# Turning 28 of 64 attention items in 32x32 blocks on VectorE, with the blocks carried through DRAM

## What is computed

```python
q_big = apply_rope(einsum('bshk,hkq->bshq', layernorm(x) @ Wq.T, w_kc_q), sin_q, cos_q)
kv_r = apply_rope(kv_c, sin_k, cos_k)
q_r = einsum('bshq,hqr->bhsr', q_big, W_qr)
k_r = einsum('bld,hdr->bhlr', kv_r, W_kr)
attn = softmax(einsum('bhsr,bhlr->bhsl', q_r, k_r), axis=-1)
ctx_c = einsum('bhsl,bld->bhsd', attn, kv_r)
ctx = einsum('bhsd,hkd->bhsk', ctx_c, w_kc_kv)       # then @ Wo.T, gate, add to x
```

## Time and profile before

| | value |
|---|---|
| median of three timed runs | 262.97 us |
| span of the profiled execution, first to last instruction | 261.0 us |
| TensorE busy | 248.7 us, 95% |
| VectorE busy | 180.5 us, 69% |
| ScalarE busy | 144.0 us, 55% |
| GpSimd busy | 136.6 us, 52% |
| share of the chain that ended last: TensorE, VectorE, GpSimd, DMA, ScalarE | 79%, 6%, 5%, 4%, 3% |

### The profile page before, as it was taken

How to read it: one execution, slowest core, us unless ns; L and a number is a source line. 1 busy time by engine, 2 the same in 40 slices (tenths; PEclk the granted TensorE clock), 3 DMA queues, 4 the chain that set the end, 5 groups by cost and what they waited for, 6 DMA issues and landing times.

```text
span 261.0 us, 5668 instructions
## 1 busy us (share of the span) xinstructions
PE 248.7 (95%) x1961; PEld 187.1 (72%) x1961; DVE 180.5 (69%) x435; ACT 144.0 (55%) x440; POOL 136.6 (52%) x221
## 2 busy tenths in 40 slices
PE   6998999999999999999999999999999999889993
PEld 6874777587776878587857876787668758666871
DVE  3799889468775858386847774777658556676575
ACT  2720566574466454746445636656655477758551
POOL 3535139642782278525744565458624952527542
PEclk9999999999999999999999999999999999999997
DMA  6986542534100250124200300030003000000112
GB/s 229 231 224 162 178 102 82 136 106 136 41 0 3 50 173 3 43 58 92 82 3 0 80 4 0 14 70 3 1 0 82 2 3 0 1 3 0 41 34 91
DMA packets 17852, 16.72 MB, mean 64 GB/s; under 512 B 5152, under 2 KB 16544, under 8 KB 17824
## 3 DMA queue, kind: packets, MB, share of 16 engines
q1 hardware_dynamic: 17184, 15.64, 22.7%
q10 hardware_dynamic: 640, 0.72, 0.9%
HBM read 11.11 MB, written 1.05 MB: 47 GB/s over the span
## 4 chain that ended last, share of the span: by engine, by line
PE 79%; DVE 6%; POOL 5%; DMA 4%; ACT 3%; issue 3%; ACTq 0%; DVEq 0%; POOLq 0%
PE ring L1124 23%; PE probs_t L1308 12%; PE scores L1297 9%; PE context L1341 9%; PE ring L1165 5%; PE ring L1090 4%; PE ring L1188 2%; PE ring L1184 2%; PE ring L1186 2%; PE ring L1151 2%; DMA w_kc_q_sb<-in_w_kc_q 2%; POOL roped L599 2%; DMA moved<-cross 2%; PE ring L1113 1%; ACT probs L775 1%
## 5 line engine op out<-in xcount | busy, mean ns | idle before, releaser
L669 POOL TENSOR_SCALAR probs<-probs,inv_sum 128x256 f32<-128x256 f32 x128 | 59.6, 478 | 87.6 <-DVE inv_sum L1028 87.5
L785 ACT COPY probs_t_sb<-probs_t 128x512 f32<-128x512 f32 x64 | 37.6, 588 | 57.7 <-PE probs_t L1308 57.7
L775 ACT ACTIVATE probs<-scores,neg_max 128x256 f32<-128x256 f32 x128 | 59.9, 478 | 4.0 <-DVE neg_max L1022 3.8
L599 POOL TENSOR_TENSOR roped<-roped,cross 128x512 f32<-128x512 f32 x30 | 37.8, 1281 | 11.5 <-DVE cross L866 11.4
L1022 DVE TENSOR_REDUCE neg_max<-scores 128x2 f32<-128x512 f32 x64 | 40.9, 680 | 2.2 <-PE scores L1297 1.9
L1124 PE MATMUL ring<-xn_hi,a_hi 128*128 128x512 f32 x96 | 40.7, 424 | 0.1
L1308 PE MATMUL probs_t<-ident,probs 128*128 128x128 f32 x256 | 40.4, 280 | 0.3 <-POOL probs L669 0.3
L1124 PE MATMUL ring<-xn_hi,a_lo 128*128 128x512 f32 x96 | 37.7, 393 | 0.0
L865 DVE TENSOR_TENSOR roped<-ring,rope_q_sb 128x512 f32<-128x512 f32 x48 | 32.8, 684 | 6.9 <-PE ring L1124 6.7
L1124 PE MATMUL ring<-xn_lo,a_hi 128*128 128x512 f32 x96 | 37.5, 391 | 0.0
L1308 PEld LDWEIGHTS probs_t<-ident,probs 128*128 128x128 f32 x256 | 28.7, 140 | 9.8 <-issue 2.2
(11 more groups left out here) (116 smaller groups left out, 464.3 us busy)
## 6 DMA issues: line engine op xcount, KB each, us to landing
moved<-cross SPq DMA_DIRECT2D x30, 128.0 KB, 2.3
wo_t_sb<-in_wo_t SPq DMA_DIRECT2D x4, 512.0 KB, 4.8
w_qr_sb<-in_w_qr SPq DMA_DIRECT2D x4, 384.0 KB, 4.3
wq_sb<-in_wq SPq DMA_DIRECT2D x3, 512.0 KB, 4.0
w_kc_q_sb<-in_w_kc_q SPq DMA_DIRECT2D x3, 384.0 KB, 4.6
x_sb<-in_x SPq DMA_DIRECT2D x3, 256.0 KB, 5.9
out<-x_sb SPq DMA_DIRECT2D x3, 256.0 KB, 2.2
wq_sb<-in_wq SPq DMA_DIRECT2D x2, 256.0 KB, 4.5
```

The costliest lines, as they stand in the source:

```text
L599: last = nc.gpsimd.tensor_tensor(roped[:, j, k, :], roped[:, j, k, :], cross[:, k, j, :], ALU.add)
L669: last = nc.gpsimd.tensor_scalar(e, e, inv_sum[:, i % 4, half:half + 1], 1.0, ALU.mult, ALU.mult)
L775: last = nc.scalar.activation(probs[:, i % E_BUFS, half, :], scores[:, i % 2, half, :], ACT.Exp, bias=neg_max[:, i % 4, half:half + 1], ac ...
L785: nc.scalar.copy(probs_t_sb[:, i % T_BUFS], probs_t[:]).then_inc(probs_t_ready, 1)
```

## The change

Of each quad of the first seven steps, the first pair (i mod 4 below 2, 28 items) is not turned on TensorE and not copied by ScalarE. Instead:

1. VectorE turns the item's 32x32 blocks within their 32 partitions, from `probs` into `x2_t` (there called `blocks_t`), one instruction of 128x512 elements, one loop after the item, right behind a reciprocal.
2. SyncE stores the pair's blocks, 512 KB, to a scratch in DRAM by four DMAs of 32 partitions each, in runs of 512 bytes.
3. When all four have landed, SyncE loads the 512 KB back by one DMA in runs of 2048 bytes, each block row now on the partition of its key, into the buffers of `probs_t_sb` that the pair would have had. There are two places in DRAM and two in `probs_t_sb`, taken in turn; from the third pair on the load also waits for the contexts that read its place before.
4. The context products wait for the load, and read their moving operand in runs of 32 elements.

```diff
+        def by_blocks(i):
+            return i % 4 < 2 and i < items - ITEMS
...
+            def send_blocks(q):
+                at = blocks_dram[q // 2 % 2].rearrange("c a (q x) -> q a c x", q=4)
+                sp.wait_ge(blocks_turned, turned_by_blocks(2 * q + 1))
+                for quarter in range(4):
+                    rows = blocks_t[BLOCK * quarter:BLOCK * (quarter + 1)]
+                    sp.dma_start(at[quarter], rows.rearrange("p c e h b -> p c (e h b)")).then_inc(blocks_out, 16)
+            def fetch_blocks(q):
+                done = turned_by_blocks(2 * q + 1) // 2
+                sp.wait_ge(blocks_out, 64 * done)
+                if done > 2:
+                    sp.wait_ge(context_ready, q - 3)
+                sp.dma_start(moved_probs[:, q // 2 % 2].rearrange("p k q e h b -> p k (q e h b)"),
+                             blocks_dram[q // 2 % 2].rearrange("(k r) a x -> (r a) k x", k=2)).then_inc(blocks_in, 16)
...
+                    if i >= 2 and by_blocks(i - 2) and i % 4 == 2:
+                        send_blocks(i // 2 - 1)
+                    pieces(steps[n][s][0])
+                    if i >= 3 and by_blocks(i - 3) and i % 4 == 3:
+                        fetch_blocks(i // 2 - 1)
...
+            def turn_blocks(i):
+                if i < 0 or not by_blocks(i):
+                    return
+                dve.wait_ge(probs_ready, i + 1)
+                if i >= 4:
+                    dve.wait_ge(blocks_out, 32 * turned_by_blocks(i - i % 4 - 1))
+                nc.vector.transpose(blocks_t[:, :, i % 2, :, :].rearrange("p c h b -> p h c b"),
+                                    probs[:, i % E_BUFS].rearrange("p h (c a) -> p h c a", a=BLOCK)
+                                    ).then_inc(blocks_turned, 1)
...
                     if i + 1 < items:
                         inverse(i + 1)
+                    turn_blocks(i - 1)
                     contexts_low(contexts_at(i))
...
             def turn_probs(i):
+                if by_blocks(i):
+                    return
                 pe.wait_ge(probs_ready, i + 1)
-                if i:
-                    pe.wait_ge(probs_t_ready, i)
+                if turned_by_array(i) > 1:
+                    pe.wait_ge(probs_t_ready, turned_by_array(i) - 1)
...
-                pe.wait_ge(probs_t_ready, 2 * q + 2)
+                if by_blocks(2 * q):
+                    pe.wait_ge(blocks_in, 8 * turned_by_blocks(2 * q + 1))
+                else:
+                    pe.wait_ge(probs_t_ready, turned_by_array(2 * q + 1))
```

More of the change, by code:

```diff
@@ L40 @@
 LEAD = 2
+BLOCK = 32
+KEY_BLOCKS = L // BLOCK
 NO_BANK = ("n", "c", "table", "move", "hand", "root", "gate", "take", "part", "pre", "half")
@@ L374, in by_halves, with turned_by_blocks, turned_by_array @@
             return i >= items - ITEMS // 2
+        def by_blocks(i):
+            return i % 4 < 2 and i < items - ITEMS
+        def turned_by_blocks(i):
+            return sum(1 for other in range(i + 1) if by_blocks(other))
+        def turned_by_array(i):
+            return i + 1 - turned_by_blocks(i)
         def half_of(i):
@@ L529, in _ @@
             first_swap = banks.index(("q", 0, 0, 1))
[L530 to L554, removed]
@@ new lines, in pieces @@
+            def pieces(slot):
+                for u, piece in slot:
+                    kind = piece[0]
+                    if kind == "q" and piece[2:] == (0, 1):
+                        sp.wait_ge(ring_free, freed[u])
+                        swap_quarters(sp, range(4) if piece[1] else (0, 1))
+                        if piece[1] == 0:
+                            late_loads()
+                            if last_merge("a", 0) <= first_swap:
+                                sp.wait_ge(ring_full, last_merge("a", 0))
+                                load_query_weights(sp, 1)
+                                load_key_weights(sp, 1)
+                        continue
+                    if kind not in ("a", "m", "o") or piece[1] + 1 == GROUPS or u + 1 != last_merge(kind, piece[1]):
+                        continue
+                    g = piece[1] + 1
+                    if u < first_swap:
+                        continue
+                    sp.wait_ge(ring_full, u + 1)
+                    if kind == "a":
+                        load_query_weights(sp, g)
+                        load_key_weights(sp, g)
+                    elif kind == "m":
+                        load_rank_weights(sp, g)
+                    else:
+                        load_output_weights(sp, g)
@@ new lines, in _ @@
+            pieces(before)
+            pieces(start)
+            for n in range(STEPS):
+                for s in range(ITEMS):
+                    i = n * ITEMS + s
+                    if i >= 2 and by_blocks(i - 2) and i % 4 == 2:
[3 more added lines that the diff above has]
+                        fetch_blocks(i // 2 - 1)
+                    pieces(steps[n][s][1])
+            pieces(after)
@@ L710, in pieces @@
                         act.wait_ge(ring_full, u + 1)
+                        if c == 0:
+                            act.wait_ge(blocks_out, 32 * turned_by_blocks(items - 1))
                         nc.scalar.copy(x2_t[:, c % 4:c % 4 + w].rearrange("p a d t -> p (a d t)"),
@@ L771, in exponentials @@
                 act.wait_ge(max_ready, i + 1)
-                if i >= E_BUFS:
-                    act.wait_ge(transposed, i - E_BUFS + 1)
+                if i >= E_BUFS and by_blocks(i - E_BUFS):
+                    act.wait_ge(blocks_turned, turned_by_blocks(i - E_BUFS))
+                elif i >= E_BUFS:
+                    act.wait_ge(transposed, turned_by_array(i - E_BUFS))
                 for half in range(2):
```

18 lines of the change are left out of this document (15 added, 3 removed).

## The result

The changed kernel takes 260.14 us in the median (259.31 to 261.6), the kernel before, run beside it, 262.98 (262.7 to 263.21): a ratio of 0.9887, 95% interval 0.9858 to 0.9915. It is faster by 2.84 us, not by the forecast 8.5. Executions more than 1.5% above the fastest of their kernel are left out of every ratio in this document, but not out of the medians. The profiled execution took 259.31 us, its span is 257.5.

A forecast was written before the change was run, and what follows sets the result against it. TensorE was taken as the bound from 34 to 222 us. 12.3 us removed, less 2.6 taken back and 1.2 waited, saves 8.5: 262.97 - 8.5 = 254.5 us, 8-in-10 range 250.8 to 262.8.

The forecast's parts named there:

- what GpSimd takes back: TensorE reaching items 3, 18, 48 and 49 and smaller places earlier, then waiting for GpSimd: 2.6 us lost.
- Removed from TensorE: On TensorE, 28 items lose four turns each, at 0.44 us per item: 12.3 us saved.
- Added to VectorE: 28 block turns at 0.68 us, 19.0 us in all; VectorE stays under TensorE, so no cost.
- The estimate of 1.24 us: Block turn on VectorE priced as four blocks by the skill page; would make the forecast 256.1 instead of 254.5 us.
- nothing queues behind that wait: On VectorE, each turn's wait for normalised rows was said to be already met, GpSimd working in order.
- Added to SyncE: Four stores and one load per pair in SyncE's queue, costed at nothing; risk: the transfer, some 2 us of queue.
- The round trip: From the reciprocal before a pair's second turn through turn, stores and load: 9.25 us, bounds 7.95 to 12.0.
- half is given back: Rival: round trip of 10.5 us, 5.6 us waits at third, sixth, tenth, thirteenth pairs' contexts; 258.9 us, chance 0.12.
- The thirteenth pair: Context products there, with a lead shrunk to 8.06 us, were the one costed wait for a load: 1.2 us.
- The range: 8-in-10 range for the whole kernel's time, leaving out slower cases and the fastest edge: 250.8 to 262.8 us.
- the forecast's own range: Likeliest case for the kernel's time: 252.3 (no load wait) to 257.6 us (round trip of 10.2); chance 0.58.
- The signs: Profile after: 144 TensorE turns, TensorE over 97% busy, turn near 0.68 us, one load wait near the thirteenth pair.

The follow-up runs named there:

- kernel 1: Against the kernel after: no block turns, stores or loads; context products of moved items read a fixed tile; 254.15 us, ratio 0.9659.
- kernel 2: Against kernel 1: VectorE's 28 block turns added, still no stores or loads; 256.95 us, ratio 0.9743.
- kernel 4: Against the kernel after: all turns, stores and loads, but contexts read a fixed tile and wait only for the previous pair's load; 257.25 us, ratio 0.9769.
- kernel 3: Against kernel 2: each block turn moved to the end of VectorE's loop, behind rope products and maxima; 254.97 us, ratio 0.9685.
- kernel 12: Against the kernel after: first, tenth, thirteenth, fourteenth pairs stay on TensorE; last rank weights behind sixth load, pairs' first turns at loop end; 259.69 us, ratio 0.9834.
- kernels 7: Against the kernel after: last group's rank weights loaded behind the sixth pair's load and the swap; 259.9 us, ratio 0.9864.
- the ninth: Against the kernel after: first, fourth, tenth, fourteenth pairs stay on TensorE; last group's rank weights behind the sixth pair's load; 258.06 us, ratio 0.9785.
- the eleventh: Against the kernel after: all fourteen pairs, last rank weights behind the sixth load, each pair's first turn at VectorE's loop end; 257.41 us, ratio 0.9754.
- kernel 6: Against the kernel after: stores of the sixth and tenth pair one loop earlier in SyncE's queue; 262.96 us, ratio 0.9942.
- 10: Against the ninth: first turn of each pair moved to the end of VectorE's loop, second turn kept; 258.43 us, ratio 0.9802.

## Why the prediction was wrong, step by step

Us saved (+) or lost (-). The medians of the first three steps are from one comparison, the last step joins two; the last context products are those of the traces.

| step of the prediction | forecast | medians | last context products | from |
|---|---|---|---|---|
| turns off TensorE, less what GpSimd takes back | 12.3 - 2.6 = +9.7 | +9.1 | +8.6 | before to 1 |
| block turn on VectorE | 0 | -2.8 | -2.2 | 1 to 2 |
| stores and loads in SyncE's queue, traffic | 0 | -0.3 | -0.7 | 2 to 4 |
| waits for loads | -1.2 | -2.9 | -2.3 | 4 to after |
| sum | +8.5 | +3.1 (+2.84 in the first comparison) | +3.4 | |

- *Removed from TensorE*: mechanism right, the term a little large. 11.2 us of busy time for 28 items is 0.40 each, not 0.44; less the 9.1 or 8.6 of the first kernel, 2.1 to 2.6 went back to GpSimd (forecast 2.6), at the places named: items 3, 18 and, for 48 and 49, item 51 (0.60, 0.37 and 1.15 us in the trace of kernel 1).
- *Added to VectorE*: the price was right, 0.69 us against the forecast 0.68. The estimate of 1.24 us was four times the 311 ns that the Trainium skill has for a 128x128 block in bf16 ("VectorE: DVE Perf Modes", section "The three transpose paths"); the trace shows it too high for this turn. The first failed step is "nothing queues behind that wait". I looked at who waits behind the wait, and not at who waits behind the instruction: the rope products, which release GpSimd, and through GpSimd rank products and turns. My own section on what is taken back had shown GpSimd without slack at several places; what a turn adds there reaches TensorE. 1.5 of the 2.2 us are shown to be this (kernel 3); 0.7 stay with VectorE's longer work, the turns' other places or the noise, not separated.
- *Added to SyncE*: this is the second failed step. I asked what stands behind the loads, and costed that at nothing, which is near (0.3 to 0.7 without the load waits). The risk that I named there is real all the same: the swap of step 3 lands later when it is issued close behind the fourth pair's load, and in kernel 12 that costs item 18 a wait of 2.65 us. I did not ask what stands ahead of the stores, nor between stores and load. At the sixth pair these were four issues of rank weights, at the tenth the swap: the stores started 0.79 and 1.81 us behind the end of the turn, and TensorE waited 1.28 and 1.87 us.
- *The round trip*: right in size where the queue was free. From the first store's issue to the load's landing it took 117.84 - 109.03 = 8.8 us at the sixth pair and 176.17 - 168.46 = 7.7 at the tenth; my sum has 8.1 for these parts. A store took 2.5 us in the median and a load 3.6, against 2.3 and 4.0 taken. The fit of the Trainium skill ("DMA: Bandwidth & Descriptors", section "Anatomy of one DMA — SWDGE (gpsimd) path") makes an estimate of 2.3 and 3.2; the trace is 0.2 and 0.4 above it. But from the end of the turn it was 9.6 and 9.5 us, with the queue ahead of the stores in it. So the sixth and tenth pair waited, two of the four that the rival "half is given back" named: its round trip of 10.5 us was met there (10.4 and 10.3 from the reciprocal), but by another cause. And even with no weights ahead, the trip at the sixth pair took 7.7, 9.4 and 10.0 us in the traces of kernels 7, 9 and 12, a spread for which the sum has one middle value.
- *The thirteenth pair*, the one forecast wait, did not wait. Its lead is 212.76 - 203.48 = 9.3 us, not the shrunk 8.06, since TensorE's wait for item 51 (1.14 us) lies inside it. The prediction had used the two turns removed there twice: as given back to GpSimd, and as a lead that shrinks. The fourteenth waits 0.36 us, and the wait for the scores behind it fell from 1.16 to 0.73, so that, as forecast, nothing comes on top there.
- *Not foreseen*: the stores' issue and landing scatter (at the sixth pair the last store landed after 2.69 us in the kernel after, 2.34 in the ninth and 4.11 in the twelfth), with them the load's start and a swap behind it, and behind some of the longer waits the granted clock is lower. That the long executions of the kernel after and of the eleventh are of this kind is likely, not shown: only those of kernels 6 and 12 were traced.
- *The range* held the time (260.14 in 250.8 to 262.8), the forecast's own range (252.3 to 257.6) did not; "half is given back", 258.9 us, was the nearest case, and had a chance of 0.12. The wide range held by its width, not by its terms.
- *The signs*: 144 turns, 0.69 us a turn and the full clock came as named. From 33.3 to 218.4 us TensorE is busy 95%, not over 97; gaps ahead of the context products came at the sixth and tenth pair, not at the third; of the named turns only that of item 18 waits, 0.77 us, under the named microsecond. One slip stands in the sum: at a round trip of 10.2 us the waits by its own rule are about 4.5 us, not 4.3, and that end of the range is 257.8; nothing hangs on it.

The best version found is the eleventh by its ratio, 0.9754, but two of its six executions took 263 us; the ninth, 0.9785, kept its four within 0.5 us. Whether a version without awaited loads in the queue ahead of a swap would keep the eleventh's time without its long executions was not tried.

## What to carry to other kernels

An instruction added to an engine with slack is not free if the next one in its queue releases an engine without slack: follow who waits for what stands *behind* it, two engines far. For a round trip through memory, write down everything that the issuing queue holds ahead of the first store, between the last store and the load, and right behind the load, at every place, and price the trip from the moment the data is ready. An experiment that takes the result's consumer away (kernel 2 against 1, kernel 4 against after) splits such a sum into its terms in a handful of runs. Where a term is smaller than the noise of the medians, compare the traces at an instruction ahead of the stretch that scatters.

## What the runs showed of the hardware that I had not expected

- A wait of TensorE can be followed by a lower clock, and then costs more than its length. Behind waits of 3.68, 2.65 and 2.00 us the granted clock averaged 0.61, 0.66 and 0.53 over the next 4.0, 5.0 and 3.6 us, by estimate 1.6 to 1.7 us lost each time; behind one of 1.87 us in the kernel after, and one of 2.14 in kernel 6, it stayed at 1.00. So the length of the wait alone does not decide it. The three are from the traces of kernels 6 and 12, both long executions.
- VectorE's turn of 128x512 elements in 32x32 blocks takes 0.69 us, as long as the maxima and the rope products over 512 elements there (0.68 us).
- A swap of four times 128 KB, issued 0.42, 0.72, 1.13, 1.20 and 1.71 us behind a load of 512 KB, landed its last part after 4.62, 3.25, 3.01, 2.59 and 2.42 us, at one place of five kernels (12, 6, 7, 11, after); three more lie at 1.47 to 1.56 us and 2.47 to 2.90. With no load ahead (9, 10) it took 2.30.
- Context products that read their operand in runs of 32 elements cost nothing more: 16 of them took 1.88 us where nothing stood ahead of them, as before the change.
